# A one-core four-layer kernel on Trainium2: every engine loop written by one helper is unrolled in Python

## The chip, the cores and the metric

One Trainium2 chip, one of its cores. The metric is the device time of one execution in microseconds (us), the median of several runs. Engines: TensorE (PE; its weight loads are listed as PEld), VectorE (DVE), ScalarE (ACT), GpSimd (POOL) and SyncE (SP, which here issues the DMAs). A "q" behind an engine's name in the trace (PEldq, DVEq) is that engine's sequencer: its register, branch and wait instructions.

## The reference, cut to what matters

Input x is 8 x 512 x 128 (batch, time, width), float32. Four layers, each an attention-like block s and a gate g:

```
for layer in 0, 1, 2, 3:
    xn = layernorm(x)
    s  = attention_of_the_layer(xn)
    g  = silu(feed_forward_of_the_layer(xn))
    x  = x + s * g
```

Layer 0: differential attention with 16 heads of 8 and a mixture of experts of which all six (4 routed, 2 shared) are computed. Layer 1: attention in which only some queries are kept, and a 64-expert mixture, computed as 34 pairs. Layer 2: a gated delta rule (a recurrence over time, done in chunks of 32 steps), and 8 experts with packed tokens. Layer 3: causal attention with a position bias, 16 heads of 64, and a gated linear unit.

## The kernel before, in words

The kernel is a list of phases. Each phase (`phase`, L43) is one block in which every engine has its own program; the engines meet through semaphores only, and a phase ends when all are done. Within a phase an engine's program is a body repeated over batches, heads, experts or chunks. It is written once as `body(i, first, last)` and repeated by `run_bodies` (L228): the first body and the last one are written out with Python integers for i, and those between are a hardware loop, `eng.Fori(1, count - 1)`, with i in a register of the engine. `first` and `last` leave out waits for work that doesn't exist yet or any more, and the filling and draining of the software pipeline.

What depends on i is of two kinds. Semaphore values: `At` (L215 to L225) keeps i * per in a register and adds a constant for each wait, so a wait in a loop body is preceded by an add on the engine's sequencer (ALU_OP in the trace). With an integer i it returns an integer. Addresses: `bass.ds(i * 2 + u, ...)` and the like, computed in registers (FUSED_REGOPS). A loop body ends with an add, a COMPARE_BRANCH and a FUSED_REGOPS, all at L231.

The order of the work inside a body is written by hand and the same for every i. Phases that matter here, with their loops:

- att0 (`attend_phase`, L407 to L719): 16 bodies of 4 groups of heads each, 14 of them in the loop. Pass 1 (L545, L547) makes scores, DVE takes their maxima (L659), pass 2 (L563, L565) makes scores again, ACT exponentiates (L628), L576 weighs the values. At the first step of a group TensorE waits for two semaphores, the group's load and a free PSUM buffer. att1 is the same function, 8 bodies.
- ex0 (`experts_phase`): 3 bodies. pairs (`pairs_phase`, L1422 to L1558): 17 bodies, 15 in the loop.
- chunks (`chunks_phase`, L2284 to L2448): 4 bodies, 2 in the loop. `blocks` (L2321) issues 64 matmuls of 32x32; each becomes two weight loads and two matmuls in the trace, 256 instructions a call, 20 calls a body.
- recur (`recur_phase`, L2451 to L2597): 8 bodies, 6 in the loop. Each is two steps of the recurrence for two groups of batches: 320 small matmuls (L2498 in `small`, L2530, L2531), 1280 TensorE instructions in the trace, in short bursts between which TensorE, DVE and ACT wait for each other.
- att3 (`layer3_attention`, L1697 to L2036): 32 bodies of two head pairs, 30 in the loop. TensorE: L1867 (output product of the item before), L1830 scores, L1840 transposes, L1815 and L1818 projections, L1857 weighing. Its waits for transposed tiles that were copied out are in `wait_copy` (L1758) and `turn`.
- some 20 short phases (norm, proj, out, lg, turn, conv, unit, out2, glu) with 2 to 6 bodies in each loop.

Three loops don't go through `run_bodies`: GpSimd's in `norm_phase` (L119), SP's in `project_phase` (L292), VectorE's in `route_phase` (L1374). Some phases (the packed experts of layer 2, the phases that choose experts, the final one) have no hardware loop at all.

Of the kernel before, what the change touches and what calls it, by code (L numbers as in the profile page):

```python
# [90 lines left out]
def norm_phase(nc, R, name, combine, second=None, store=None):  # L91

    with phase(nc, name) as p:
# [19 lines left out]
        with nc.Block() as block:  # L114
# [12 lines left out]
            @block.scalar  # L127
            def _(act):
                def body(i, first, last):
                    if combine:  # L130
                        for u in range(2):
                            n = i * 2 + u
                            if not first:

                                act.wait_ge(s_dve, scaled(act, i, 2 * per))
                            nc.scalar.activation(ex[:, u], R.f[:, bass.ds(n * QT, QT), :].rearrange("p a d -> p (a d)"),
                                                 ACT.Silu).then_inc(s_exp, 1)
                    for u in range(2):
                        n = i * 2 + u
                        for v in range(NV):  # L140

                            act.wait_ge(s_pT, scaled(act, n, NV, v + 1))
                            if v == 0:
                                nc.scalar.activation(R.xnT[:, bass.ds(n * T, T)], pT[:, (v + u * NV) % 2], ACT.Copy).then_inc(s_xT, 1)
                            else:
                                nc.scalar.activation(R.xn2T[:, bass.ds(n * T, T)], pT[:, (v + u * NV) % 2], ACT.Identity,
                                                     bias=second[1], scale=second[0]).then_inc(s_xT, 1)

                run_bodies(act, B // 2, body)

            @block.tensor
            def _(pe):
                def body(i, first, last):
                    for u in range(2):
                        n = i * 2 + u
                        for v in range(NV):
                            pe.wait_ge(s_xn, scaled(pe, n, NV, v + 1))
                            if not (first and u * NV + v < 2):
                                pe.wait_ge(s_xT, scaled(pe, n, NV, v - 1))
                            for j in range(QT):  # L160
                                ins = nc.tensor.transpose(pT[:, (v + u * NV) % 2, j * P:(j + 1) * P],
                                                          (xm if v else xn)[:, u, j], R.ident[:, :])
                            ins.then_inc(s_pT, 1)

                run_bodies(pe, B // 2, body)

            @block.vector
            def _(dve):
                c = Chain(dve, s_dve, per)

                def body(i, first, last):
                    for u in range(2):
# [36 lines left out]
                        c.over()  # L209

                run_bodies(dve, B // 2, body)

# [13 lines left out]

def run_bodies(eng, count, body):  # L228

    body(0, True, False)  # L230
    with eng.Fori(1, count - 1) as i:  # L231
        body(i, False, False)
    body(count - 1, False, True)

# [3027 lines left out]
```

## Time and profile before

| what | value |
|---|---|
| median of 3 runs | 4967.24 us (4958.47 to 4968.73) |
| the profiled execution's own time | 5000.41 us |
| its span, first to last instruction | 4998.4 us |
| mean granted TensorE clock | 0.847 |
| instructions recorded | 110868 |
| PE / PEld / DVE / ACT / POOL busy | 3769.8 / 2195.0 / 2816.7 / 2049.2 / 999.6 us |

### The profile page before, as it was taken

Reading aid. Unit: us, or ns where it says so; the run is one execution under the profiler, and the core shown is the slowest. Engines: PE = TensorE matmul, PEld = TensorE weight load, DVE = VectorE, ACT = ScalarE, POOL = GpSimd, SP = SyncE. Lnnn points to the kernel's source line nnn. Section 1 sums busy time; section 2 is a strip of 40 time slices with the busy share of each in tenths; the row PEclk is TensorE's granted clock in tenths of the full one; section 3 lists DMA queues with packets and bytes.
Section 4 is the critical chain, followed back from the end, with each engine's and each line's share of the span. In section 5 each row is a group of like instructions: output and inputs, shape, how many; then the busy total and the mean of one; then the engine's idle time right before and its main releaser. Section 6 shows DMA issues by size and latency. Waiting matters only on the chain. (4 is left out here: it accounts for less than half of the span.)

```text
span 4998.4 us, 110868 instructions
## 1 busy us (share of the span) xinstructions
PE 3769.8 (75%) x37428; PEld 2195.0 (44%) x37428; DVE 2816.7 (56%) x7044; ACT 2049.2 (41%) x4247; POOL 999.6 (20%) x1324
## 2 busy tenths in 40 slices
PE   4699999749975999735999943455447339999998
PEld 1244444337752222123666621135446226666665
DVE  5577777641134888655555554843543355555554
ACT  4366666513333677612222212221102125555553
POOL 0000000000000000002666530600001514444441
PEclk9799999859986999957999966566558669999999
DMA  3322111100002211000000001010000413333331
GB/s 99 66 51 50 49 48 48 30 9 10 9 1 63 44 43 39 20 4 11 15 15 15 15 23 40 32 55 29 4 4 2 49 64 111 110 109 109 110 110 33
DMA packets 179786, 218.22 MB, mean 44 GB/s; under 512 B 36509, under 2 KB 154852, under 8 KB 179182
## 3 DMA queue, kind: packets, MB, share of 16 engines
q1 hardware_dynamic: 175470, 206.76, 14.4%
q0 software_dynamic: 4096, 8.40, 1.1%
q8 instruction: 154, 2.52, 0.2%
q14 instruction: 66, 0.54, 0.0%
HBM read 162.16 MB, written 34.60 MB: 39 GB/s over the span
## 5 line engine op out<-in xcount | busy, mean ns | idle before, releaser
L628 ACT ACTIVATE att_E<-att_pX,att_gs 128x512 f32<-128x512 f32 (+3 forms) x1536 | 844.9, 580 | 416.5 <-PE att_pX L565 288.3
L659 DVE TENSOR_REDUCE att_mx<-att_pS 128x1 f32<-128x512 f32 (+3 forms) x1536 | 812.4, 546 | 202.5 <-PE att_pS L547 136.3
L545 PE MATMUL att_pS<-att_ks,att_qs 72*128 72x512 bf16 (+4 forms) x1536 | 524.0, 342 | 116.6 <-DVE att_mx L659 51.7
L563 PE MATMUL att_pX<-att_qs,att_ks 75*128 75x512 bf16 (+4 forms) x1536 | 507.6, 332 | 55.8 <-ACT att_E L628 54.8
L1789 POOL TENSOR_TENSOR att_E<-att_E,att_rz 128x128 f32<-128x128 f32 (+3 forms) x512 | 357.5, 719 | 465.9 <-DVE att_rz L1995 465.9
L545 PEld LDWEIGHTS att_pS<-att_ks,att_qs 76*128 76x128 bf16 (+1 forms) x1536 | 149.3, 97 | 575.0 <-DVE att_mx L659 480.3
L1482 POOL TENSOR_TENSOR pairs_h<-pairs_c,pairs_r 128x512 f32<-128x512 f32 x272 | 344.8, 1270 | 191.4 <-DVE pairs_c L1542 190.5
L1529 ACT ACTIVATE pairs_r<-pairs_ph 128x512 f32<-128x512 f32 x272 | 162.4, 597 | 438.7 <-PE pairs_pc L1500 435.8
L1542 DVE TENSOR_TENSOR pairs_c<-pairs_pc,pairs_r 128x512 f32<-128x512 f32 x272 | 188.1, 692 | 254.8 <-ACT pairs_r L1529 253.9
L576 PE MATMUL att_pO<-att_E,att_vs 128*9 128x512 f32 (+3 forms) x3072 | 323.6, 493 | 1.6 <-ACT att_E L628 1.6
L1927 ACT ACTIVATE att_E<-att_S,att_nm 128x128 f32<-128x128 f32 (+3 forms) x512 | 281.5, 552 | 80.9 <-DVE att_nm L1989 80.8
L1508 PEld LDWEIGHTS pairs_po<-pairs_a,pairs_h 128*128 128x128 f32 x2176 | 286.2, 192 | 42.2 <-POOL pairs_h L1482 3.2
L1989 DVE CUSTOM_DVE_ANT_0 att_S<-att_pS,att_bias 128x128 f32<-128x128 f32 (+3 forms) x512 | 230.4, 487 | 106.6 <-PE att_pS L1830 94.2
L1508 PE MATMUL pairs_po<-pairs_a,pairs_h 128*128 128x128 f32 x2176 | 287.0, 275 | 2.3 <-POOL pairs_h L1482 2.3
L1498 PE MATMUL pairs_ph<-xnT,pairs_a 128*128 128x512 f32 x544 | 280.1, 597 | 5.0 <-POOL pairs_sb L1470 5.0
L527 POOL COPY att_gs<-att_gains 128x2 f32 (+3 forms) x96 | 18.5, 193 | 1241.8 <-PE att_pO L576 1241.5
L1196 PEld LDWEIGHTS ex_po<-ex_a,ex_h 128*128 128x128 f32 x1536 | 202.1, 192 | 91.8 <-issue 91.0
L563 PEld LDWEIGHTS att_pX<-att_qs,att_ks 79*128 79x128 bf16 (+1 forms) x1536 | 150.0, 98 | 200.9 <-ACT att_E L628 122.8
L547 PE MATMUL att_pS<-att_mb 128*128 128x128 bf16 x1024 | 229.2, 224 | 0.0
L565 PE MATMUL att_pX<-att_mb 128*128 128x128 bf16 x1024 | 226.7, 222 | 0.0
L1222 ACT ACTIVATE ex_h<-ex_ph,ex_bs 128x512 f32<-128x512 f32 x192 | 131.9, 687 | 214.8 <-PE ex_ph L1187 214.8
L1238 DVE SCALAR_TENSOR_TENSOR f<-ex_po,ex_ws,f 128x128 f32<-128x128 f32 x192 | 54.0, 344 | 278.1 <-PE ex_po L1196 278.1
(421 smaller groups left out, 6912.9 us busy)
## 6 DMA issues: line engine op xcount, KB each, us to landing
att_bias<-in_bias_dram SPq DMA_DIRECT2D x64, 896.0 KB, 4.4
parts<-proj_part SPq DMA_DIRECT2D x144, 128.0 KB, 2.3
att_xb<-xnT SPq DMA_DIRECT2D x64, 256.0 KB, 2.6
att_qs<-parts SPq DMA_DIRECT2D x192, 64.0 KB
att_ks<-parts SPq DMA_DIRECT2D x192, 64.0 KB
att_w<-in_w3a_dram SPq DMA_DIRECT2D x64, 192.0 KB, 2.4
att_qs<-parts SPq DMA_DIRECT2D x96, 96.0 KB
att_ks<-parts SPq DMA_DIRECT2D x96, 96.0 KB
```

The source lines that it names most:

```text
L545: ins = nc.tensor.matmul(pS[:, r % 2, :w], qs[:K1, u, x, j * P:(j + 1) * P], ks[:K1, u, x, :w], start=True, stop=not causal)
L547: ins = nc.tensor.matmul(pS[:, r % 2, w - P:w], mb[:, 2], mb[:, 0], start=False, stop=True)
L563: ins = nc.tensor.matmul(pX[:, s % 2, :w], ks[:, g % NB, x, kt * P:(kt + 1) * P], qs[:, g % NB, x, q0(kt):], start=True, stop=not causal)
L576: ins = nc.tensor.matmul(pO[32 * x:32 * x + DV, g % 2, q0(kt):], vs[:, g % 2, x // maps, kt], E[:, kt % 2, x, :w], start=(kt == 0), stop=( ...
L628: nc.scalar.activation(E[:, kt % 2, x, :w], pX[:, s % 2, :w], ACT.Exp, scale=gs[:, g % 2, x // maps:x // maps + 1]).then_inc(s_e, 1)
L659: V.reduce_max(mx[:, h % NB, r:r + 1], pS[:, r % 2, :w1(r % QT)], AX.X).then_inc(s_mx, 1)
L1482: nc.gpsimd.tensor_tensor(h[:, g % 2], c[:, g % 2], r[:, g % 2], ALU.mult).then_inc(s_h, 1)
L1498: nc.tensor.matmul(ph[:, g % 2], a[:, v, 0], R.xnT[:, b * T:(b + 1) * T], start=True, stop=True)
L1508: ins = nc.tensor.matmul(po[:, g % 2, q * P:(q + 1) * P], h[:, g % 2, q * P:(q + 1) * P], a[:, v, 1], start=True, stop=True)
L1789: nc.gpsimd.tensor_tensor(E[:, k, :width(j)], E[:, k, :width(j)], rz[:, u, k:k + 1].broadcast_to([P, width(j)]), ALU.mult).then_inc(s_n, 1)
L1927: nc.scalar.activation(E[:, k, :width(j)], S[:, r % RING, :width(j)], ACT.Exp, bias=nm[:, u, k:k + 1], scale=-1.0, accum_out=Z[:, u, k:k + ...
L1989: nc.vector.tensor_tensor_reduce(out=S[:, r % RING, :w_], in0=pS[:, r // 2 % 2, h, :w_], in1=bias[:, u, off:off + w_], scale=-1.0 / DW, sc ...
```

## The change

`run_bodies` repeats the body in Python, so that i is an integer in every body: all semaphore values and addresses become constants, and the branches go. `first` and `last` are true for the same bodies as before, so each engine has the same work, waits and order.

```
--- before.py
+++ after.py
@@ -227,10 +227,8 @@
 
 def run_bodies(eng, count, body):
 
-    body(0, True, False)
-    with eng.Fori(1, count - 1) as i:
-        body(i, False, False)
-    body(count - 1, False, True)
+    for i in range(count):
+        body(i, i == 0, i == count - 1)
```

## Rows read from the trace of the kernel before

**Rows 1.** The page: busy time of TensorE, and the instruction queues (packets, MB, share).

```profile
PE 3769.8 (75%) x37428; PEld 2195.0 (44%) x37428; DVE 2816.7 (56%) x7044; ACT 2049.2 (41%) x4247; POOL 999.6 (20%) x1324
...
q8 instruction: 154, 2.52, 0.2%
```

**Rows 2.** Busy time by window, with count, clock, DMA share, GB/s: att0 twice, pairs, att3.

```profile
core 0: us, PE busy (x) PEld busy (x) DVE busy (x) ACT busy (x) POOL busy (x), PEclk, DMA share, GB/s
...
877.50:902.20 24.70, 22.45 (x204) 10.83 (x205) 18.79 (x55) 16.90 (x34) 0.73 (x4) 1.00 0.20 49
926.75:951.60 24.85, 22.59 (x204) 10.87 (x204) 18.91 (x55) 16.80 (x34) 0.73 (x4) 1.00 0.15 26
...
2841.19:2876.20 35.01, 35.01 (x195) 23.55 (x193) 20.68 (x33) 9.55 (x16) 21.03 (x18) 1.00 0.06 15
2876.20:2908.00 31.80, 31.80 (x174) 21.09 (x173) 19.21 (x30) 8.36 (x14) 18.60 (x16) 1.00 0.03 9
...
4628.70:4653.80 25.10, 25.05 (x194) 15.77 (x192) 14.70 (x57) 14.68 (x45) 11.18 (x16) 1.00 0.34 110
```

**Rows 3.** Instructions of L231, L658 and L543: duration ns min/median/max; the second in 3590 to 3600.

```profile
L231 PEldq COMPARE_BRANCH  x116: 67/208/3891, 27.1 to 4965.7; - x116
...
L231 PEldq COMPARE_BRANCH  x1: 3891/3891/3891, 3593.9 to 3593.9; - x1
...
L658 DVEq ALU_OP  x1260: 40/40/45, 237.1 to 2042.3; - x180
...
L543 PEldq EVENT_SEMAPHORE  x14: 51/51/51, 173.9 to 2057.6; - x14
```

**Rows 4.** chunks, first body (written out): a window, and instruction packets in 3451 to 3500.

```profile
3458.20:3461.80 3.60, 1.93 (x127) 1.79 (x128) 1.91 (x3) 0.00 (x0) 0.00 (x0) 0.50 0.02 5
...
q8 instruction: 13, 0.21, 1.9%
```

**Rows 5.** chunks: timeline of ACT at the start of bodies 1, 2 and 3.

```profile
3509.93 0.60 ACT L2368 ACTIVATE chunks_brow<-chunks_pR 128x512 f32<-128x512 f32 x1 [11.89 <-PE chunks_pR L2339]
...
3600.07 0.60 ACT L2368 ACTIVATE chunks_brow<-chunks_pR 128x512 f32<-128x512 f32 x1 [12.77 <-PE chunks_pR L2339]
...
3688.36 0.60 ACT L2368 ACTIVATE chunks_brow<-chunks_pR 128x512 f32<-128x512 f32 x1 [11.77 <-PE chunks_pR L2339]
```

**Rows 6.** recur by body (0, 1, 4, 7); instruction packets in 3776.3 to 3817.4; DMA in 3829.6 to 3875.6.

```profile
3776.30:3797.50 21.20, 14.81 (x635) 13.43 (x639) 4.63 (x12) 4.26 (x15) 3.81 (x16) 0.74 0.02 4
3797.50:3817.40 19.90, 12.80 (x657) 11.48 (x649) 4.60 (x12) 4.72 (x17) 3.08 (x13) 0.92 0.02 5
...
3841.20:3852.80 11.60, 10.70 (x640) 9.67 (x641) 4.55 (x12) 4.66 (x17) 3.08 (x13) 1.00 0.00 0
...
3875.60:3892.80 17.20, 12.48 (x649) 11.17 (x640) 4.54 (x12) 3.86 (x12) 0.86 (x4) 0.90 0.02 4
...
q8 instruction: 10, 0.16, 1.8%
...
DMA packets 0, 0.00 MB, mean 0 GB/s; under 512 B 0, under 2 KB 0, under 8 KB 0
```

**Rows 7.** att3, timeline of PE: a half body in the loop, the same in the last body.

```profile
4641.22 1.16 PE L1867 MATMUL att_pA<-att_wo,att_oT 128*128 x8
...
4648.48 0.44 PE L1840 MATMUL att_pT<-ident,att_E 128*128 128x128 f32 x2
...
4892.15 1.16 PE L1867 MATMUL att_pA<-att_wo,att_oT 128*128 128x128 f32 x8
...
4899.26 0.44 PE L1840 MATMUL att_pT<-ident,att_E 128*128 128x128 f32 x2
```

**Rows 8.** proj0, timeline of PE: the same step in three successive bodies.

```profile
94.18 1.11 PE L324 MATMUL proj_pvt<-ident,proj_vT 128*128 128x128 f32 x4 [2.70 <-ACT proj_vT L362]
...
114.96 1.12 PE L324 MATMUL proj_pvt<-ident,proj_vT 128*128 128x128 f32 x4 [2.74 <-ACT proj_vT L362]
...
135.25 1.12 PE L324 MATMUL proj_pvt<-ident,proj_vT 128*128 128x128 f32 x4 [2.65 <-ACT proj_vT L362]
```

## The prediction

> **What bounds the kernel now.** First the page: TensorE is the busiest engine with 3769.8 us, 75% of the span [rows 1]. An average over such unlike phases decides little, so next the windows. In the big phases TensorE is at its limit: 35.00 of 35.00 us busy in pairs, 25.05 of 25.10 in att3, 22.45 of 24.70 in att0 [rows 2]. Register and branch work there can only matter where it delays TensorE. Third, the loop's own instructions by line: a wait's add takes 40 ns on VectorE's sequencer, a loop's branch on TensorE's a median of 208 ns, with one of 3891 ns [rows 3]. The reader should see that such work mostly runs ahead on the sequencers while the engines compute.
>
> The best view is a comparison that the kernel carries within itself. Each phase's first and last bodies are already written out with constants, as the change writes all of them. So the last body next to a loop body, up to the step where the pipeline starts to drain, prices the edit phase by phase. And the first bodies show what written-out code costs that loop code doesn't: it must be fetched. Fetching is visible as 16 KB packets on queue q8. In the first body of chunks TensorE does some 128 matmuls and 128 loads, 256 instructions, in 3.60 us, but is busy for 1.93 us of them, and over a longer stretch 13 packets arrive in 49 us, one in 3.8 us [rows 4]. So one packet goes with 256 instructions, and here TensorE waits for the next one each time, about 2 us. In recur the bodies that arrive for the first time take 21.20 and 19.90 us, with 10 packets; the body that goes round in the loop takes 11.60 us with the same 640 matmuls, and in 46 us of it not one DMA packet of any kind is recorded; the last body, new again, takes 17.20 us [rows 6].
>
> **The change, part by part.** The sum is made against the profiled execution, 5000.4 us; the runs shown have a median of 4967.2, which is 33 us (0.7%) less, and I carry the difference over unchanged.
>
> 1. *recur, the loop gone.* Bodies 2 to 6 run from code already on the engine now and will have to be fetched like body 1. Each goes from 11.60 to 19.90 us: 5 x 8.3 = +41.5 us. The last body now starts with some of its code there; it loses that, 17.20 to an estimated 19 us, +1.8. Together +43. From below: 5 packets a body (1280 instructions) at the 3.60 us of chunks [rows 4] give 18.0 us, +34 in all; from above body 0's 21.20 us gives 5 x 9.6 + 4 = +52. I take body 1, since it is the same steady-state code.
>
> 2. *Fetching elsewhere.* It is hidden wherever 256 TensorE instructions take much longer than 3.8 us. att0 has 409 matmuls and loads in 24.70 us, so 256 in 15 us; att3 386 in 25.10, 17 us; pairs 387 in 35.00, 23 us [rows 2]. That cover is four to six times the packet's pace. Nothing. If the cover failed, each packet would cost up to 2 us as in chunks; that is a rival below. chunks' bodies (over 5000 instructions) come in as packets already, in the loop too.
>
> 3. *chunks, the branch.* The one branch of 3891 ns, at 3593.9 us, ends body 1 [rows 3]. From the start of body 1 to that of body 2 ACT needs 90.14 us, from 2 to 3 88.29 us [rows 5], without a branch back. Gain 1.8 us; from below 0 (the branch hides in a fetch that comes anyway), from above its full 3.9 us.
>
> 4. *att3, waits and registers.* From the output product to the second transpose of step 2 a loop body takes 7.26 us, the last one 7.11 [rows 7]: -0.15 us per half body, 60 halves, -9.0. TensorE is the bound here, so it counts in full. From below 0, from above -0.3 per half (the remainder of the half gains as much), -18. TensorE's branch at 208 ns hides behind the matmuls already queued.
>
> 5. *att0.* The windows are cut at ACT's first exponential of a group. Two groups take 24.70 us in a loop body and 24.85 in the last [rows 2]: constants are slower here by 0.15, and nothing else differs but fewer loads in flight (share 0.15 for 0.20). 28 such pairs of groups, +4.2 us. I take the step that grows to be a group's first, where two waits stand together: with constants one of them is an instruction of its own, 51 ns, which only written-out bodies have [rows 3]. From below -4 (the sum of the branch and register work returns), from above +8. att1, the same code, I put at 0.
>
> 6. *pairs.* The window over the last loop body has 195 matmuls in 35.01 us, the written-out one after it 174 in 31.80, both 5.5 per us, and TensorE is busy throughout [rows 2]. Nothing.
>
> 7. *Short phases.* A body of proj0 takes 20.78 us in the loop and 20.29 written out [rows 8], -0.49. Here the engines wait for each other, so adds lie on the path. TensorE runs 116 loop bodies in all [rows 3]; less att0 14, att1 6, pairs 15, att3 30, ex0 1, chunks 2, recur 6, some 42 are in short phases. Between 0 and 0.49 each; half of it, 42 x 0.245 = -10.3. Range -3 to -20.
>
> Sum: +43.3 - 1.8 - 9.0 + 4.2 - 10.3 = +26 us. Profiled 5026, median **4993 us**, 0.5% slower.
>
> A page speaks against item 1. The Trainium skill ("Runtime: NRT & Kernel Launch", Instruction fetch mechanics) says that the sequencer fetches the next 16 KiB while it executes the current one, that crossing a boundary is mostly hidden, and that a taken branch outside the window is what stalls, so that full unrolling is preferred. By that rule item 1 would be nothing, and the sum -17 us. For code that TensorE runs through this fast the trace disagrees [rows 4, 6]; for the rest it leaves the rule standing [rows 2].
>
> **The rivals.** *Fetch keeps ahead in recur* (the other side, faster): the slow first bodies would then be a start-up cost of the phase, and the rest of the sum, -17 us, is left: 4950. It decides if packets in recur come closer than the 2.3 us that a fifth of an 11.60 us body allows. Against it: the last body is as new to the engine and slow, 17.20 us, though everything around it is in swing [rows 6].
>
> *The gains cancel it*: recur at its lower bound +34, att3 -18, chunks -4, short phases -15, att0 0: -3 us, 4964. For it speaks that each comparison in 4 and 7 covers only part of a body.
>
> *Fetch also stalls the big phases*: att3's DMA share is 0.34 and its code would now come in beside it [rows 2]. At 2 us for every second one of its 44 packets (30 bodies of 25.1 us, one packet in 17 us), att3 alone adds 44: 5037. Against it: the written-out window of pairs and the last body of att3 keep or beat the loop's pace [rows 2, 7].
>
> *It doesn't do what it says*: constants are turned into registers again or code size is handled in another way, and nothing moves: 4967. The written-out bodies in this very trace speak against it. The three loops outside the helper stay in any case.
>
> **How the numbers follow.** My case 0.62; fetch ahead 0.12; cancelled 0.13; big phases stalled 0.08; no effect 0.05. About 0.2%, 10 us, is what a measurement can tell from no change. My own case's terms vary by some 12 us around 4993 in quadrature, a little of it below 4977. Slower: 0.62 + 0.08 = 0.70; the same 0.13 + 0.05 = 0.18; faster 0.12. The range takes in my case's bounds and the cancelled and no-effect cases and leaves out most of the fetch-ahead and the stalled ones: 4962 to 5022.
>
> **What would show it.** q8 packets rise from 154 to about 300 (74856 TensorE instructions and some waits, by 256). recur takes about 160 us in place of 116.5, eight bodies of 19 to 20 us with a packet each 3.8 to 4 us and "issue" gaps of 2 us. A half body of att3 takes about 12.4 us in place of 12.55, two groups of att0 24.85 us, a body of pairs 35.0. No branch of 3.9 us. A recur body near 11.6 us, or gaps of 2 us in att0 or att3, would prove me wrong.

## The result and the profile after

The changed kernel takes 4988.14 us (median of 6 runs, 4980.84 to 4999.69) where the one before took 4962.93 beside it (6 runs, 4958.47 to 4968.73): ratio 1.0052, 95% interval 1.0038 to 1.0066, 25 us slower. Its profiled execution took 4988.87 us. The first fence is the changed kernel's page, against [rows 1]: 147 more instruction packets on q8, and 98093 instructions instead of 110868, for the adds and branches are gone.

```profile
span 4987.1 us, 98093 instructions
PE 3755.8 (75%) x37373; PEld 2190.4 (44%) x37428; DVE 2808.7 (56%) x7044; ACT 2041.6 (41%) x4247; POOL 1003.5 (20%) x1324
...
q8 instruction: 301, 4.93, 0.4%
```

Next the windows over bodies 1, 2, 4 and 7 of recur in the changed kernel (columns as in [rows 2]), against [rows 6]. Every body now looks like the one that used to arrive for the first time.

```profile
3784.00:3803.70 19.70, 12.61 (x652) 11.11 (x645) 4.63 (x12) 4.66 (x16) 3.29 (x14) 0.91 0.02 5
3803.70:3822.70 19.00, 12.50 (x658) 11.53 (x651) 4.73 (x12) 4.66 (x16) 2.89 (x13) 0.91 0.02 4
3841.50:3859.80 18.30, 11.25 (x652) 9.86 (x644) 4.54 (x12) 4.66 (x16) 3.00 (x13) 1.00 0.02 5
3899.60:3919.50 19.90, 13.25 (x645) 12.00 (x644) 4.63 (x12) 3.86 (x12) 0.77 (x3) 0.83 0.02 4
```

Where TensorE's extra 7 to 8 us go is seen in its waits over bodies 1 to 7, 3784 to 3919 us (us in total, times, longest), and in the instruction packets of 115.6 us of the same stretch:

```profile
PE recur_pO L2528 <- issue: 19.1, 13, 2.0
PE recur_pA L2496 <- issue: 8.8, 6, 1.8
PE recur_pS L2496 <- issue: 8.3, 7, 1.6
PE recur_pU L2496 <- issue: 6.4, 6, 1.4
PE recur_pA L2496 <- POOL recur_st L2484: 0.9, 1, 0.9
```

```profile
q8 instruction: 31, 0.51, 1.8%
```

The 32 waits "issue" are 42.6 us in 135 us, 1.3 us each. 31 packets came in the 115.6 us of bodies 1 to 6, one in 3.73 us, and at that pace 36 in the 135: nearly one such wait for each packet. The waits are 6.1 us a body; in the rest of the extra time TensorE is busy for longer, 12.4 us a body on average against the 10.70 of [rows 6], at a mean granted clock of 0.93 against 1.00 (11.25 us in body 4, at 1.00).

The same trace has the start and end of each packet, and they fit the waits one by one. Two such waits, timeline of TensorE:

```profile
3843.38 0.87 PE L2496 MATMUL recur_pA<-recur_S,recur_st 32*32 32x64 f32 x48 [1.41 <-issue]
...
3847.05 0.91 PE L2496 MATMUL recur_pS<-recur_U,recur_st 32*32 32x64 f32 x49 [1.00 <-issue]
```

In bodies 1 to 6 there are 29 pauses of over 0.6 us between the starts of TensorE's matmuls and loads. Each ends 1.22 to 1.51 us after the end of a q8 packet, and from one to the next TensorE starts exactly 256 instructions, its sequencer's included (512 in two of the 28 cases). So TensorE has run through its 256 instructions before the next 256 are there. The pace is a round trip, and not a rate of transfer: a packet takes 1.07 us on average, TensorE resumes some 1.4 us after it, and the next packet starts some 1.3 us after that.

In att3 the steps of [rows 7] now lie 7.10 us apart, 4644.08 to 4651.18, where the loop body took 7.26 (timeline of TensorE):

```profile
4644.08 1.16 PE L1865 MATMUL att_pA<-att_wo,att_oT 128*128 128x128 f32 x8
...
4651.18 0.44 PE L1838 MATMUL att_pT<-ident,att_E 128*128 128x128 f32 x2
```

**The profiled execution of the kernel before was disturbed.** It took 5000.41 us, 37 above the median of its kernel. With the two executions lined up by the start of each VectorE instruction, out2 took some 31 us less in the changed kernel. That looked like a gain of written-out code, and experiment 1 shows that it isn't.

A single pair of executions scatters by some us in the short phases and in chunks. The table therefore goes by all profiled executions of this study in which a stretch has the code of the one kernel or of the other. Experiments 5, 9, 10 and 12 swap two waits in att0 and att1 and are left out of the first three rows. It is worked out from the starts of VectorE's instructions in the traces; in us, lowest to highest, and the difference of the means. The last row leaves out out2 where it stalled (the first execution of the kernel before, experiments 9 and 12).

| stretch | loops (executions) | written out (executions) | difference |
|---|---|---|---|
| att0's loop | 739.6 to 742.2 (4) | 743.7 to 744.0 (6) | +3.6 |
| att0's tail, out0 | 110.0 to 111.3 (4) | 105.6 to 109.8 (6) | -4.3 |
| att1 | 388.8 (4) | 389.6 (6) | +0.8 |
| ex0 | 322.3 (4) | 322.3 (10) | 0.0 |
| pairs | 564.7 (4) | 564.4 to 566.5 (10) | +0.6 |
| chunks | 343.3 to 349.2 (4) | 335.9 to 342.2 (6) | -6.8 |
| recur | 122.1, 125.2 | 160.0, 162.0 | +37.3 |
| att3 | 765.2 to 765.4 (4) | 758.0 (10) | -7.2 |
| all others together | | | -10.1 |

The sum is +13.9 us, below the 25.2 of the medians (19 to 33 by the interval of the ratio). The pair of undisturbed spans, 4962.4 and 4987.1, gives +24.7. The last column is good to 0.1 us in ex0, att1 and att3 and to several us in the others; what of the remaining 11 us is such scatter is not settled.

### The profile page after: what moved, and what is told of

Its sections match the earlier page's. It is cut to its first block and busy times, and to the rows that moved or that the text cites. A ratio compares the mean times of both kernels' runs of the same rounds, so it can differ in the third digit from the quotient of the medians.

```text
span 4987.1 us, 98093 instructions
## 1 busy us (share of the span) xinstructions
PE 3755.8 (75%) x37373; PEld 2190.4 (44%) x37428; DVE 2808.7 (56%) x7044; ACT 2041.6 (41%) x4247; POOL 1003.5 (20%) x1324
## 5 line engine op out<-in xcount | busy, mean ns | idle before, releaser
L543 PE MATMUL att_pS<-att_ks,att_qs 72*128 72x512 bf16 (+4 forms) x1536 | 522.8, 341 | 120.6 <-DVE att_mx L657 52.3
L543 PEld LDWEIGHTS att_pS<-att_ks,att_qs 76*128 76x128 bf16 (+1 forms) x1536 | 149.2, 97 | 575.3 <-DVE att_mx L657 456.4
L525 POOL COPY att_gs<-att_gains 128x2 f32<-128x2 f32 (+1 forms) x96 | 18.7, 195 | 1249.5 <-PE att_pO L574 1249.2
```

The lines of the kernel that those rows point to most:

```text
L543: ins = nc.tensor.matmul(pS[:, r % 2, :w], qs[:K1, u, x, j * P:(j + 1) * P], ks[:K1, u, x, :w], start=True, stop=not causal)
```

## The experiments

Unless said otherwise a time is given by its ratio to runs of the kernel before on the same chip.

**1. The kernel before, once more.** No edit.

> The kernel before, unchanged, for a second profiled execution. The first one's own time was 5000.4 us, 37 us above the median of six runs (4962.9), and its phase out2 took 139.5 us from the last product of recur to its end, against 108.8 in the changed kernel, with VectorE and ScalarE idle for 27 and 56 us in bodies that are a hardware loop. Theory A (a disturbance of that one execution): out2 takes about 109 us here and the profiled execution's own time is near 4965. Theory B (the loop's code is what stalls, behind the 64 gathers of GpSimd): out2 takes about 139 us again, and the changed kernel gained those 30 us, so that its other losses must be nearer 55. In recur a resident body takes 11.6 us by both.

4964.45 us, and out2 took 113.1 us instead of 139.5, near the changed kernel's 108.8. That fits theory A, on one execution. The windows from recur's last product to out2's end, of this execution, of the disturbed one and of the changed kernel:

```profile
3888.40:4001.50 113.10, 45.11 (x160) 32.99 (x160) 71.34 (x125) 32.03 (x59) 71.25 (x66) 0.65 0.38 77
```

```profile
3894.30:4033.80 139.50, 42.38 (x160) 29.60 (x160) 67.85 (x114) 31.89 (x59) 64.21 (x65) 0.64 0.42 62
```

```profile
3921.10:4029.90 108.80, 38.89 (x160) 27.55 (x160) 68.01 (x113) 31.75 (x59) 68.86 (x65) 0.71 0.52 80
```

TensorE has the same 160 products in all three, and no engine is busy for longer in the long one than in experiment 1. The long one comes back in experiments 9 and 12, where out2's code is written out, so it doesn't hang on the loop.

**2. TensorE's loop in recur put back, everything else as changed.**

```
--- changed kernel, recur_phase, TensorE
-                run_bodies(pe, NBODY, body)
+                body(0, True, False)
+                with pe.Fori(1, NBODY - 1) as i:
+                    body(i, False, False)
+                body(NBODY - 1, False, True)
```

> The changed kernel with a hardware loop put back for TensorE in recur alone (one of 55 loops); the other three engines of recur keep their constants. Theory (TensorE's code must be fetched at about 3.9 us for each 256 instructions, 1280 a body): bodies 2 to 6 fall back to 11.6 us, recur to about 117 us from 152, and the time to 4988 - 35 = 4953 us, ratio to before 0.998. Rival 1 (the fetching of VectorE, ScalarE and GpSimd counts as well): bodies fall only to 14 to 16 us, 4965 to 4975. Rival 2 (constants in waits of the other engines are slower or faster, not the fetch of TensorE): no change from 4988.

4936.61 us, ratio 0.9955 (0.9939 to 0.9972). One loop of 55 is worth 48 us by the two ratios, nearly twice the whole loss and more than the 35 that was expected. recur fell to 117.0 us, 43 less than in the changed kernel and 5 less than in experiment 1. The window over a resident body, TensorE's waits over 51 us of such bodies, the packets in 42 us of them, and the branches:

```profile
3814.05:3825.35 11.30, 10.70 (x643) 9.67 (x644) 4.54 (x12) 4.66 (x17) 3.07 (x13) 1.00 0.00 1
```

```profile
PE recur_pA L2502 <- POOL recur_st L2490: 1.1, 4, 0.3
```

```profile
q14 instruction: 2, 0.02, 0.1%
```

```profile
L232 PEldq COMPARE_BRANCH  x6: 76/210/238, 3790.9 to 3847.3; - x6
```

The "issue" waits are gone, q8 brings nothing, and the branch back takes 210 ns. Rival 1, that the other engines' written-out code counts too, falls: the body takes 11.30 us, less than the 11.60 with all engines in loops. Rival 2 falls with the 48 us.

**3. The other way round: the kernel before with TensorE's loop in recur written out.**

```
--- kernel before, recur_phase, TensorE
-                run_bodies(pe, NBODY, body)
+                for i in range(NBODY):
+                    body(i, i == 0, i == NBODY - 1)
```

> The kernel before with one change of the 55: TensorE's loop in recur written out. Theory: every body of recur takes 18 to 20 us, recur 152 instead of 116.5 us, ratio to before 1.007 (4998 us), q8 instruction packets up by 25 to about 179. Rival (the loss in the changed kernel needs the other engines' constants or the many written-out phases ahead): ratio 1.000 to 1.002.

Ratio 1.0089 (1.0073 to 1.0106), 5004.38 us; recur 161.9 us, q8 179 packets, as expected to the packet. The theory's 1.007 lies just below the interval: recur alone, 39.8 us more than in experiment 1, would make 1.0080. Writing out this one loop costs more than writing out all 55, so the other 54 bring a gain.

**4. A loop whose body is too long.** TensorE's bodies 1 to 6 of recur as three rounds of a loop over two bodies; the rest as before.

```
-                with pe.Fori(1, NBODY - 1) as i:
-                    body(i, False, False)
+                with pe.Fori(0, (NBODY - 2) // 2) as j:
+                    body(j * 2 + 1, False, False)
+                    body(j * 2 + 2, False, False)
```

> The kernel before, where TensorE's loop in recur goes round 3 times over a body written twice (2560 instructions instead of 1280); waits still compare with registers. Fetch theory, if 2560 instructions are too many to stay on the engine: bodies 2 to 6 cost 18 to 20 us like written-out ones, plus up to 3.9 us for each of the two branches taken: ratio to before 1.007 to 1.009. Fetch theory, if they do stay: body 2 is slow (one more 8 us), bodies 3 to 6 at 11.6: ratio 1.001 to 1.002. Rival (constants in place of registers are what slows recur): all loop bodies at 11.6 us, ratio 1.000.

Ratio 1.0090 (1.0070 to 1.0110). Waits compare with registers here just as in the kernel before, and the bodies cost what written-out ones do. The windows over the first two rounds, and the branches (of the two that the trace has in these 500 us):

```profile
3797.38:3841.75 44.37, 26.92 (x1282) 24.00 (x1282) 9.08 (x24) 9.66 (x33) 6.94 (x27) 0.85 0.02 5
3841.75:3885.58 43.83, 26.38 (x1280) 23.55 (x1281) 9.15 (x24) 9.29 (x32) 6.17 (x24) 0.85 0.02 4
...
L2539 PEldq COMPARE_BRANCH  x2: 4674/4755/4836, 3836.7 to 3880.4; - x2
```

44 us for two bodies: a branch of 4.7 to 4.8 us to code that is no longer there, and 19.5 to 19.8 us for each body, where a written-out one takes 19.2 on average. Packets arrive all the time, 24 on q8 in these 88 us. So it is residence that counts, not constants against registers.

**5. The order of two waits in att0 and att1**, in the changed kernel (the same swap in pass 2).

```
                     if r == 0:
-                        pe.wait_ge(s_in[u], at(NL, NL * (h // NB + 1)))
                     if not (early and r < 2):
                         pe.wait_ge(s_mx, of(at, IT, h, r - 1))
+                    if r == 0:
+                        pe.wait_ge(s_in[u], at(NL, NL * (h // NB + 1)))
```

> The changed kernel with two pairs of waits swapped in att0 and att1: where TensorE waits for a group's load and for a free PSUM buffer at once, the free buffer (the one that comes last) is now written first or second the other way round. In the changed kernel every group of att0 takes 12.36 us, in the one before half of them took 12.28; att1's took 14.41 against 14.33 or so. Theory (with constants one of the two waits becomes an instruction of its own of 51 ns, and it is the late one, so that 51 ns and a dispatch lie on the path): the groups of att0 that took 12.28 us return to 12.28, -0.08 on about 30 groups = -2.4 us or, if all of them gain, -4.8. Rival (the constants shift the phase of the pipeline in another way): groups stay at 12.36. The whole time cannot tell these apart, the profile can.

att0's loop took 738.9 us instead of 744.0, att1 387.6 instead of 389.6: 7.1 us together, and the execution 4975.5 us. The windows over two groups of att0 and the separate wait instructions between 150 and 2060 us, of the changed kernel, then of this one:

```profile
448.99:473.70 24.71, 22.39 (x203) 10.79 (x204) 18.79 (x55) 16.82 (x34) 0.73 (x4) 1.00 0.24 50
```

```profile
L541 PEldq EVENT_SEMAPHORE  x93: 51/51/51, 175.7 to 2047.0; - x93
```

```profile
444.17:468.73 24.56, 22.38 (x204) 10.75 (x203) 18.79 (x55) 16.80 (x34) 0.73 (x4) 1.00 0.24 50
```

```profile
L547 PEldq EVENT_SEMAPHORE  x96: 51/51/51, 162.1 to 2049.3; - x96
```

Nearly as many such instructions stand in both. What moved is the semaphore: with constants, the wait that is written second becomes the separate instruction. L541 is the wait for the free buffer, which comes last; L547 the one for the load, which has long landed. 0.15 us for two groups, as the prediction read from the last body; how much of it belongs to each of the two swapped pairs was not tried.

**6. A small loop in chunks**, on top of experiment 2.

```
-                    for l in range(NL):
+                    with pe.Fori(0, NL) as l:
                         for u in range(2):
-                            pe.wait_ge(s_T, at(2 * NL, 2 * l + u + 1))
+                            pe.wait_ge(s_T, pe.snap(l * 2 + (i * 2 * NL + u + 1)))
                             pe.nop(nofuse=True)
-                            blocks(pK[:, u], Lm[:, u, l % 2], X[:, u]).then_inc(s_Y, 1)
+                            blocks(pK[:, u], Lm[:, u], X[:, u]).then_inc(s_Y, 1)
...
+                        dve.wait_ge(s_Y, at(2 * NL, 2 * l + u + 1))
```

> The changed kernel with TensorE's loop put back in recur (as in the run of 4936.6 us) and a new, small loop in chunks: the four levels of a body, 1024 TensorE instructions each, go round in a hardware loop inside the written-out body, so that levels 1 to 3 run from code that is already there. To have the same addresses in every level there is one buffer Lm for each u instead of two, and VectorE waits for the product that reads it. Fetch theory: a level that arrives takes about 15 us (1024 instructions, 4 packets at 3.85), a resident one is set by TensorE's 6.4 us, two copies and three VectorE steps of about 0.6 us for each u, an estimated 8 to 10 us: 12 resident levels x -6 = -60 to -85 us. With recur: 4855 to 4880 us, ratio to before 0.980 to 0.984. Rival 1 (chunks is bound by the exchange between TensorE, ScalarE and VectorE, and not by the fetch): 0 to -10 us, 4930. Rival 2 (the taken branches cost 4 us each time, as in the loop of two bodies): -12 x 6 + 12 x 4 = -24, 4912.

4834.88 us, ratio 0.9746 (0.9732 to 0.9760), 102 us below experiment 2 and more than expected, because a resident level takes 6.2 us and not 8 to 10. The windows over two levels of the changed kernel, then over two resident ones of this kernel:

```profile
3551.50:3567.30 15.80, 8.14 (x551) 7.61 (x553) 3.95 (x6) 1.19 (x2) 0.00 (x0) 0.50 0.02 4
3567.30:3583.00 15.70, 7.50 (x511) 6.96 (x505) 3.38 (x5) 1.19 (x2) 0.00 (x0) 0.50 0.02 4
```

```profile
3516.60:3522.20 5.60, 4.97 (x510) 4.78 (x499) 3.44 (x6) 1.22 (x3) 0.00 (x0) 0.92 0.01 3
3522.20:3528.40 6.20, 4.81 (x512) 4.65 (x512) 3.95 (x7) 1.19 (x3) 0.00 (x0) 1.00 0.00 0
```

Same matmuls, same copies. The streamed level also runs at half the granted clock (0.50, 1.2 GHz), where TensorE is idle for half of each stretch; the resident one gets 1.00. Of the 9.5 us between the two, 2.7 are TensorE's longer busy time (7.50 against 4.81), the rest are waits. This loss was in the kernel before as well, where the body of chunks was a loop of over 5000 instructions.

**7 and 8. Half the instructions.** recur's operands in bfloat16 (less precise), one pass for each matmul, 640 TensorE instructions a body: in 7 written out, in 8 with TensorE's loop.

```
-        st = p.sb("st", [P, 4, 5, HALF, C])
-        S = p.sb("S", [P, 2, 2, HALF, HV])
+        st = p.sb("st", [P, 4, 5, HALF, C], BF16)
+        S = p.sb("S", [P, 2, 2, HALF, HV], BF16)
...
```

> The changed kernel, all loops written out, where recur's operands (the copied chunks, S, U, R) are bfloat16 instead of float32, so that a matmul is one pass and not two: 640 TensorE instructions a body instead of 1280, 2.5 packets. The precision of layer 2 is lower. Fetch theory: 2.5 packets x 3.9 = 9.8 us of fetch, about as long as the body's own chain, so that bodies take 10 to 12 us and recur 85 to 100 us, ratio to before 0.992 to 0.996. Rival (the written-out body is slow for its constants, or by a fixed delay in each of its waits): the bodies stay at 17 to 20 us, 4980.

> The same bfloat16 recur with TensorE's loop put back in it: 640 resident instructions a body. Fetch theory: the fetch was nearly covered in the written-out bfloat16 version, so this gains at most 1 to 2 us a body on it, against 7 to 8 us a body in float32: 0 to -12 us. Rival (written-out code costs the same 8 us a body whatever its number of instructions): -40 to -50 us.

7: ratio 0.9903 (0.9887 to 0.9919), 4911.87 us, recur 91.7 us. 8: 0.9873 (0.9858 to 0.9889), 4899.22 us, recur 77.3. Putting the loop back takes 14.4 us off recur here, against 43.0 in float32; a resident body takes 7.8 us, a written-out one 10.7 on average. The granted clock is 0.50 all through recur in both, so it is not what parts them. A fixed loss for each written-out body would have left the 40 to 50 us of the rival; the loss falls with the number of instructions, and by more than the half, as expected where much of the fetch is covered. 7's bodies and recur came out as expected (10 to 12 and 85 to 100 us), but its ratio lies below the expected 0.992 to 0.996: that was worked out from a written-out recur of 152 us, where the changed kernel's takes 160.0. The 12.7 us between the medians are just over the bound of 12 for 8; 10.7 us is more than 2.5 packets at 3.73.

**9 and 12. The best version**, twice: experiment 6 with the waits of experiment 5, and recur's TensorE loop over bodies 1 to 7.

```
-                with pe.Fori(1, NBODY - 1) as i:
-                    body(i, False, False)
-                body(NBODY - 1, False, True)
+                with pe.Fori(1, NBODY) as i:
+                    body(i, False, False)
```

> The version with TensorE's loops in recur and in the levels of chunks (4834.9 us), the swapped pairs of waits in att0 and att1, and recur's last body taken into the loop, since TensorE does the same work in it. Fetch theory: the last body of recur costs 11.6 us or less instead of some 17, about -6; the waits give 0.08 us on each of some 90 groups, -7 us: 4822 us, ratio to before 0.972. Rival (the pieces don't add up, since the time of a piece is given back at the next wait): 4835.

> The best version once more (TensorE's loops in recur and in the levels of chunks, the waits swapped), since its first timing (ratio 0.9733, 0.9703 to 0.9763) was scattered, with 4828 to 4860 us. Theory: 4822 us against 4960, ratio 0.972, that is 0.0025 below the version without the swapped waits and with the last body of recur outside the loop (0.9746). Rival (those two pieces bring nothing): 0.9746. The interval will hardly part the two; the profile shows the pieces.

0.9733 (0.9703 to 0.9763) and 0.9718 (0.9684 to 0.9752): faster than both kernels, with medians of 4849.00 and 4845.16 us, but not told apart from experiment 6; the 4822 us that were expected were not reached. By the traces the pieces are there: recur 110.6 and 111.7 us instead of 114.2, att0's loop 740.1 and 739.8 instead of 744.0, att1 387.6 instead of 389.6. But the executions scatter on these chips (4829 to 4860, and 4825 to 4858; the kernel before 4956 to 4999, and 4957 to 5003), and in both profiled ones the stall in out2 is back. Who waits in it, in experiment 9, and the queue of the gathers in 130 us around it:

```profile
PEld out_py L2665 <- DVE out_gt L2716: 79.4, 5, 53.8
...
ACT out_sg L2680 <- remote: 53.6, 1, 53.6
DVE s L2722 <- DMA parts<-proj_part: 44.0, 2, 35.7
```

```profile
q0 software_dynamic: 2048, 4.20, 33.0%
```

VectorE waits for a load that SyncE issued while the queue of GpSimd's gathers has a third of the DMA time. That the two collide is a guess, and the gathers alone don't do it: the same 2048 packets ran in the out2 of the changed kernel, 39.5% of the DMA time of its 109 us, without a stall. Why it strikes in some executions only wasn't tried.

**10 and 11. How much code stays.** 10: chunks' bodies 1 to 3 a loop too, around the loop of the levels, on experiment 9. 11: two rounds of a loop over three bfloat16 bodies of recur.

```
+                with pe.Fori(1, NBODY) as i:
+                    body(i, False, False)
```

```
+                with pe.Fori(0, (NBODY - 2) // 3) as j:
+                    for e in range(3):
+                        body(j * 3 + (e + 1), False, False)
```

> The same, where the bodies 1 to 3 of chunks are a hardware loop of TensorE again, around the loop of the levels. One such body is about 2110 TensorE instructions of code (1024 before the levels, 32 of transposes, 1024 for a level, and waits). 1280 stayed on the engine in recur, 2560 did not. If 2110 stay: bodies 2 and 3 take 5 x 6.2 us and some 8 us for the start, about 39 us instead of 61, -44 us: 4778 us. If they don't: two taken branches of 4.7 us as in the loop of two bodies, +9 us: 4831, and the level's own code, 1024, must still give levels of 6.2 us.

> How much code stays on TensorE: recur in bfloat16 (640 instructions a body), where TensorE's loop goes round twice over a body written three times, some 1950 instructions. 1280 stayed, about 2110 and 2560 did not. If 1950 stay: the branch back takes 208 ns and bodies 4 to 6 take 7.7 us as in the resident bfloat16 loop, bodies 1 to 3 9.6 us or so. If they don't: the branch takes 3.3 to 4.8 us and bodies 4 to 6 take 9.6 us again.

Neither stayed. 10 gave 0.9784 (0.9755 to 0.9812), a median of 4870.13 us, with chunks at 251.3 us against experiment 9's 238.3; 11 took 4919.57 us, where bodies 4 to 6 took 13.5, 9.0 and 11.7 us. The branches of 10 (outer loop, inner loop), then those of 11:

```profile
L2363 PEldq COMPARE_BRANCH  x3: 76/3327/3887, 3525.6 to 3657.7; - x3
...
L2352 PEldq COMPARE_BRANCH  x16: 76/216/242, 3443.9 to 3657.5; - x16
```

```profile
L2539 PEldq COMPARE_BRANCH  x2: 83/2024/3964, 3800.9 to 3834.7; - x2
```

3.3 to 4.0 us where the body is about 2100 (10) or 1984 (11) recorded instructions long, waits included, 0.2 us where it is 1032. In all three rows the shortest, 76 or 83 ns, is the branch not taken at the end.

## Why the prediction was right

Predicted 4993 us, measured 4988.14, with the sign and the mechanism as told. That +26 met the +25 of the medians so closely is partly luck: the terms as measured add up to +13.9, for recur costs less than forecast and chunks and the short phases gain more. Of its signs, q8 has 301 packets (about 300 predicted), a half body of att3 takes 12.43 us (12.4), and bodies 1 to 7 of recur 18.3 to 20.8 (19 to 20). The "issue" gaps are 1.3 us on average and 2.0 at most, where 2 were predicted. From TensorE's first product to its last, as the prediction counted 116.5 us, recur takes 152.6 and not 160; the 160.0 of the table has wider bounds, in which the kernel before takes 122 to 125. By its steps:

- *Item 1, recur.* Predicted +43.3, measured +37.3, between the lower bound of 34 and the estimate. The term was over-sized by taking body 1, 19.90 us, for all: from body 2 to 6 they took 95.8 us, 19.2 each, where those of experiment 1 took 11.5. Also body 0, put at no change, took 16.5 us by VectorE's instructions where the four executions with loops have 20.3 to 21.7; why is open. Packets came every 3.73 us, nearer to the 3.60 of [rows 4]. Experiments 2 and 3 show the cause from both sides, 4 excludes the constants, 7 and 8 tie the loss to the number of instructions.
- *The page against item 1.* The rule of the Trainium skill ("Runtime: NRT & Kernel Launch", Instruction fetch mechanics), that crossing a boundary is mostly hidden and full unrolling is preferred, agrees with ex0, pairs and att3 and fails in recur. The rival that rested on it, 4950 us, falls with the waits at each packet. Its other half, that a taken branch outside the window stalls, agrees with experiments 4, 10 and 11, at 3.3 to 4.8 us; but where it puts the window at two pages, five packets of code (1280 instructions) branch back in 0.21 us in experiment 2, and the measurement decides.
- *Item 2, fetching elsewhere.* Right within 1 us: ex0 0.0, pairs +0.6. The rival of stalls in the big phases falls, since att3 got faster.
- *Item 3, the branch in chunks.* The step was under-sized: -1.8 predicted, with at most the branch's own 3.9 us, measured -6.8. One branch of 3351 ns stands in experiment 1's chunks too; what the other 3 us are was not tried, and the single executions scatter by 6 us here.
- *Item 4, att3.* -9.0 predicted, -7.2 measured: a half body takes 12.43 us instead of 12.55, while the steps of [rows 7] alone gained 0.16.
- *Item 5, att0.* +4.2 predicted, +3.6 measured, or +4.3 without experiment 1, one of whose first groups had 2.8 us of its own. Experiment 5 confirms the step (two waits, the late one an instruction of its own). att1, put at 0 though it has the same code, lost 0.8.
- *Item 6, pairs.* Nothing predicted, +0.6.
- *Item 7, short phases.* -10.3 predicted; att0's tail with out0 and all others give -14.4, inside the bounds.
- *The base.* The sum was made against an execution that was 37 us long for a reason of its own, and the difference was carried over. It did no harm, since the disturbed stretch was in none of the terms. The rival in which the gains cancel recur was nearer than its chance said: by the table's terms it lacked 14 us, by the medians 25.

## What to carry to other kernels

Before a loop is written out, divide TensorE's instructions by 256 and ask in what time it gets through that many: under the 3.7 us measured here it waits at each such block, 1.3 us a time in recur. Keep such code in hardware loops with short bodies (some 1030 and 1300 instructions with their waits stayed, 1984 and more didn't), also inside a body that is otherwise written out. Code that runs slower can be written out: it gained 7 us in att3 and cost 4 us in att0, until the waits were swapped. Where two waits then stand together, write the one that comes last first.

## What the runs showed of the hardware that was not expected

- A level of chunks, 1024 instructions, takes 6.2 us from resident code (code that is already on the engine) and 15.7 us streamed, at a granted clock of 1.00 and 0.50. This larger loss was in both kernels, and it was not seen in the prediction. With a small loop chunks takes 237 us instead of 340.
- A taken branch of TensorE costs about 210 ns to resident code and 3.3 to 4.8 us otherwise.
- Code arrives one packet of 256 instructions after the other, one in 3.73 us, though a packet takes only 1.07 us: TensorE's pauses end 1.22 to 1.51 us after a packet, and the next packet starts some 1.3 us later.
